# Pass one of a two-layer FFT-attention block: plain fp32 transforms in row halves of the array, one more pipeline stage, softmax taps finished on GpSimd

## The reference

```python
def _autocorrelation(Q, K, V):            # H = 8 heads, per channel
    qf = jnp.fft.fft(q, axis=2)
    kf = jnp.fft.fft(k, axis=2)
    corr = jnp.fft.ifft(qf * jnp.conj(kf), axis=2).real
    w, idx = jax.lax.top_k(corr.transpose(0, 1, 3, 2), 8)   # int(2 * log(64)) = 8 lags
    w = jax.nn.softmax(w, axis=-1)
    for i in range(8):
        g = jnp.minimum(idx[:, :, None, :, i] + pos, L - 1)
        out = out + w[:, :, None, :, i] * jnp.take_along_axis(v, g, axis=2)
...
x = x + _L0_xattn_ref(_layernorm(x), ctx, ctx)
x = x + _L0_ffn_ref(_layernorm(x), lora_A, lora_B, W, bias, lora_weights)   # W plus 8 LoRA adapters
x = x + _L1_xattn_ref(_layernorm(x), ctx, ctx, ...)  # grouped softmax attention
x = x + _L1_ffn_ref(_layernorm(x), ...)              # MLP plus routed low-rank experts
```

## Time and profile before

| | |
|---|---|
| three runs | 796.23, 796.25 and 799.37 us, median 796.25 |
| profiled execution | span 795.4 us, 13302 instructions; a time of its own is not listed, the median lies 0.85 us above the span |
| busy over the span | TensorE 91%, VectorE 66%, ScalarE 65%, GpSimd 44% |
| pass one | 0 to 273 us |
| first Q transforms of tiles 0, 1, 2, 3 | start at 9.56, 35.92, 64.39 and 77.94 us |
| DMA | 45.93 MB, 58 GB/s over the span, up to 401 GB/s in 2 us slices at the start |

### The profile page before, as it was taken

How to read it: one execution, slowest core, us unless ns; L and a number is a source line. 1 busy time by engine, 2 the same in 40 slices (tenths; PEclk the granted TensorE clock), 3 DMA queues, 4 the chain that set the end, 5 groups by cost and what they waited for, 6 DMA issues and landing times.

```text
span 795.4 us, 13302 instructions
## 1 busy us (share of the span) xinstructions
PE 727.3 (91%) x4048; PEld 550.2 (69%) x4048; DVE 521.6 (66%) x1265; ACT 520.6 (65%) x953; POOL 348.6 (44%) x430
## 2 busy tenths in 40 slices
PE   3779999999998765889999999999999999999983
PEld 2546767676765553667778778788788788786772
DVE  3367999999998346656666666666666665665422
ACT  4446786767674377867867867867867866866110
POOL 3054684444442214334544544544544544535323
PEclk9799999999999968999999999999999999999998
DMA  6751433232212221011011011011011011000000
GB/s 169 232 93 41 146 120 94 66 92 66 92 59 74 73 76 62 32 40 36 19 54 37 16 53 40 13 53 40 13 53 40 13 53 40 22 19 14 14 14 27
DMA packets 30464, 45.93 MB, mean 58 GB/s; under 512 B 7488, under 2 KB 9792, under 8 KB 30432
## 3 DMA queue, kind: packets, MB, share of 16 engines
q1 hardware_dynamic: 30432, 45.53, 19.1%
HBM read 37.13 MB, written 8.39 MB: 57 GB/s over the span
## 4 chain that ended last, share of the span: by engine, by line
PE 82%; DVE 5%; ACT 4%; issue 4%; POOL 1%; DMA 1%; SPq 0%; POOLq 0%; DVEq 0%; ACTq 0%
PE bank L1036 14%; PE bank L1038 13%; PE bank L1037 13%; PE wide L1036 6%; PE wide L1038 5%; PE wide L1037 5%; PE bank L1245 3%; PE wide L1134 3%; PE bank L1109 3%; PE wide L1335 2%; PE bank L1269 2%; PE wide L1146 2%; DMA gate_raw<-in_L_ffn_gate_w 1%; PE bank L1225 1%; PE wide L1199 1%
## 5 line engine op out<-in xcount | busy, mean ns | idle before, releaser
L636 POOL TENSOR_TENSOR va<-mv,small 128x1 f32<-128x1 f32 x80 | 15.3, 192 | 211.0 <-DVE mv L1016 98.4
L428 ACT ACTIVATE q_stack<-qt_h 32x512 fp32r<-32x512 f32 x128 | 80.6, 630 | 1.9
L1036 PE MATMUL bank<-down_h,ht_h 128*128 128x512 f32 x128 | 53.6, 419 | 4.8 <-DVE ht_l L940 3.4
L948 DVE RECIPROCAL y<-bank 128x256 f32<-128x256 f32 x32 | 56.0, 1751 | 0.0
L706 POOL TENSOR_TENSOR kbd_b<-kt_h,small 128x512 bf16<-128x512 f32 x32 | 34.1, 1088 | 48.0 <-ACT kt_h L550 48.0
L971 DVE TENSOR_TENSOR x<-bank,x_res 128x512 f32<-128x512 f32 x16 | 11.1, 692 | 66.9 <-PE bank L1038 66.9
L1036 PE MATMUL wide<-up_h,t_h 128*128 128x512 f32 x128 | 53.0, 414 | 1.1 <-DVE t_l L927 1.1
L720 POOL TENSOR_TENSOR y_l<-y,y_h 128x512 fp32r<-128x512 f32 x16 | 20.6, 1290 | 72.9 <-ACT y_h L580 72.9
L1037 PE MATMUL wide<-up_l,t_h 128*128 128x512 f32 x128 | 51.2, 400 | 0.0
L1038 PE MATMUL wide<-up_h,t_l 128*128 128x512 f32 x128 | 51.1, 400 | 0.0
L1038 PE MATMUL bank<-down_h,ht_l 128*128 128x512 f32 x128 | 51.0, 398 | 0.0
(11 more groups left out here) (217 smaller groups left out, 2361.5 us busy)
## 6 DMA issues: line engine op xcount, KB each, us to landing
ctx_t<-in_ctx SPq DMA_DIRECT2D x32, 256.0 KB, 2.8
x_in<-in_x SPq DMA_DIRECT2D x16, 256.0 KB, 2.7
x_res<-in_x SPq DMA_DIRECT2D x16, 256.0 KB, 3.4
x_rows<-x SPq DMA_DIRECT2D x16, 256.0 KB, 3.5
x_in<-x_rows SPq DMA_DIRECT2D x16, 256.0 KB, 2.6
x_res<-x_rows SPq DMA_DIRECT2D x16, 256.0 KB, 3.5
out<-stage SPq DMA_DIRECT2D x16, 256.0 KB, 2.0
stage<-in_L_ffn_up_w SPq DMA_DIRECT2D x2, 1024.0 KB, 4.9
```

The costliest lines, as they stand in the source:

```text
L428: last = act.activation(out[STACK * part:STACK * (part + 1), p, :], halves[STACK * p:STACK * (p + 1), :].bitcast(F32), ACT.Copy)
L948: dve.reciprocal(y[:, :, b, :], part[:, 1]).then_inc(S["den_s"], 1)
L1036: pe.matmul(out_ps, w_hi, m_hi, start=start, stop=False)
```

## The change

Pass one is written anew around these edits; pass two keeps its code.

- **Transforms.** `transform` becomes two plain fp32 matmuls, one for each sequence: sequence b has its data and its DFT matrix on rows 64b to 64b+63 and writes a PSUM bank of its own. Q, K, V and W need one such pair each. The splits x_h, x_l, c_h, c_l, wt_h, wt_l, dft_h, dft_l are gone, and so are the second K transform and the block-diagonal matrices. Q and W write ps_a, K and V write ps_b (two banks each). qf, prod and prod2 are instructions over both sequences, 1024 or 2048 wide. corr is eight matmuls of 64 columns in place of eight of 128.
- **One stage more.** x1(i) instead of x1(i+1) is made in body(i), the FFN is that of i-1, x2 is finished and stored in body(i) for tile i-2. x1 gets three buffers, x2 and vf two. The loop is unrolled and runs to NT+1.
- **Taps on GpSimd.** `match_replace` writes 0 over the kept weights after exp; GpSimd subtracts this from the weights and multiplies by 1/total.
- **Residual and bias.** x2 = FFN + x1 + b0 is two adds on GpSimd; the identity matmul and x1b are gone.
- **Loads.** ctx_t is read by the transforms themselves: SP loads tile i+3 in body(i) after v_ps. The order of SP's body is now: store of x2(i-2), x_res(i+1), x_in(i+4), weights, ctx_t(i+3).
- **Weights.** The host hands over W, fc1, expert_w and the LoRA matrices transposed and laid out, and the LoRA loads (four in place of fourteen) go out first. w0 = W.T (loaded) + A x B on VectorE; rt is split over bodies -1 and 0.

The diff, cut to its core:

```diff
 # SP
+            sp.dma_start(a_raw[:], lora_a).then_inc(S["lora_in"], 16)
+            sp.dma_start(b_raw[:], lora_bt).then_inc(S["lora_in"], 16)
+            sp.dma_start(coef[:], lora_w).then_inc(S["lora_in"], 16)
+            sp.dma_start(w0_sum[:], w0_t.rearrange("(c p) o -> p c o", p=P)).then_inc(S["lora_in"], 16)
...
             def body(i):
                 if early(i):
                     load2(0)
+                t = i - 2
+                if live(t):
+                    sp.wait_ge(S["x2_s"], t + 1)
+                    sp.dma_start(rows(x2_rows, t), x2s[t % 2][:]).then_inc(x2_stored[t % 2], 16)
                 t = i + 1
                 if live(t):
                     wait(sp, S["x1_s"], t)
                     sp.dma_start(x_res[:], rows(x_rows, t)).then_inc(S["res_loaded"], 16)
-                t = i - 1
-                if live(t):
-                    sp.wait_ge(S["x2_s"], t + 1)
-                    sp.dma_start(rows(x2_rows, t), x2[:]).then_inc(S["x2_stored"], 16)
...
-                    sp.wait_ge(S["x_hi"], t)
+                    sp.wait_ge(S["xn1_s"], t)
                     sp.dma_start(x_in[:], rows(x_rows, t)).then_inc(S["x_loaded"], 16)
...
-                t = i + 4
-                if live(t):
-                    sp.wait_ge(S["c_lo"], t)
+                t = i + 3
+                if live(t) and t > 0:
+                    sp.wait_ge(S["v_ps"], t)
                     sp.dma_start(ctx_t[:], rows(ctx_rows, t)).then_inc(S["ctx_loaded"], 16)
 # TensorE
-                return split_product(out_ps[:], dft_h[:, w], dft_l[:, w], hi[:], lo[:], True, True)
+                for b in range(2):
+                    k = slice(SEQ * b, SEQ * (b + 1))
+                    last = pe.matmul(out_ps[:, D * b:D * (b + 1)], dft[k, col:col + P], src[k, :], start=True, stop=True)
+                return last
...
+                t = i + 2
+                    pe.wait_ge(S["xn1_s"], t + 1)
+                    wait(pe, S["prod2_s"], t - 1)
+                    transform(ps_a, Q0, xn1).then_inc(S["q_ps"], 1)
+                    pe.wait_ge(S["ctx_loaded"], 16 * (t + 1))
+                    wait(pe, S["vsw_s"], t)
+                    transform(ps_b, K0, ctx_t).then_inc(S["k_ps"], 1)
+                # o(i); corr(i+2); transposes of wgt(i+1); V(i+2); W(i+1); FFN(i-1); transposes of xn2(i)
 # ScalarE, in this order: x1t_h(i-1), qf(i+2), wt(i+1), xn2(i), a weight's cast, vf(i+2),
 # exp(i+2), xn1(i+3), two half-partition copies of vf(i+2) (vsw_s), x2(i-1) (x2_raw)
 # GpSimd
             def body(i):
+                t = i + 1
+                if live(t):
+                    pool.wait_ge(S["rep_s"], t + 1)
+                    pool.wait_ge(S["exp_s"], t + 1)
+                    wait(pool, S["wt_ps"], t)
+                    pool.tensor_tensor(wgt[:], weight[:, :, 0:SEQ], kept_not[:], ALU.subtract).then_inc(S["sub_s"], 1)
+                    pool.wait_ge(S["sub_s"], t + 1)
+                    pool.wait_ge(S["inv_s"], t + 1)
+                    pool.tensor_tensor(wgt[:], wgt[:], total_inv[:].unsqueeze(2).to_broadcast([P, 2 * DC, SEQ]), ALU.mult
+                                       ).then_inc(S["wgt_s"], 1)
+                t = i
+                if live(t):
+                    wait(pool, S["xn2_s"], t)
+                    normaliser(t, mv2, va2, rs2, nm2, nb2, 2)
+                t = i + 3
+                if live(t):
+                    wait(pool, S["xn1_s"], t)
                     normaliser(t, mv1, va1, rs1, nm1, nb1, 1)
                 if staged_before(i):
                     low_half(i - 1, 0)
                     low_half(i - 1, 1)
...
+                t = i - 2
+                if live(t):
+                    x2_t = x2s[t % 2]
+                    pool.wait_ge(S["x2_raw"], t + 1)
+                    pool.tensor_tensor(x2_t[:], x2_t[:], x1[t % 3][:], ALU.add).then_inc(S["x2_res"], 1)
+                    pool.wait_ge(S["x2_res"], t + 1)
+                    pool.tensor_tensor(x2_t[:], x2_t[:], b0_all[:], ALU.add).then_inc(S["x2_s"], 1)
 # VectorE, in this order: match_replace, total, total_inv of i+1; prod(i+2); x1t_l(i-1);
 # x1(i), bn_stats, bn_aggr; bn_stats, bn_aggr of x_in(i+3); max, shift of i+2; prod2(i+1)
+                    w = ps_a[:].rearrange("p (b n) -> p b n", b=2).unsqueeze(2).to_broadcast([P, 2, 2, D])
+                    dve.tensor_tensor(prod2[:], w, vf[t % 2][:].rearrange("p j b n -> p b j n"), ALU.mult
+                                      ).then_inc(S["prod2_s"], 1)
```

More of the change, by code:

```diff
@@ new lines, in body @@
+                    for c in range(2 * DC):
+                        top = dve.max(m8[:, c, :], corr[:, c, :])
+                    top.then_inc(S["tops_s"], 1)
+                    dve.wait_ge(S["tops_s"], t + 1)
+                    wait(dve, S["sub_s"], t)
+                    best = m8[:, :, 0:1]
+                    dve.tensor_tensor(weight[:, :, 0:SEQ], corr, best.to_broadcast([P, 2 * DC, SEQ]), ALU.subtract)
+                    dve.tensor_tensor(weight[:, :, SEQ:], m8[:], best.to_broadcast([P, 2 * DC, TOP]), ALU.subtract
+                                      ).then_inc(S["shift_s"], 1)
@@ L1102, in body @@
-                t = i + 2
-                if live(t):
-                    pe.wait_ge(S["prod_s"], 2 * (t + 1))
-                    wait(pe, S["rep_s"], t)
-                    for c in range(DC):
-                        k = slice(c * P, (c + 1) * P)
-                        for j in range(2):
-                            last = pe.matmul(bank[4][:, k], prod[:, j, k], icorr[j], start=(j == 0), stop=(j == 1))
-                    last.then_inc(S["corr_ps"], 1)
-                    transform(bank[V_BANK[0]], V0, c_h, c_l).then_inc(S["v_ps"], 1)
+                    pe.wait_ge(S["xn1_s"], t + 1)
@@ L1116, in body @@
-                    for c in range(DC):
-                        last = pe.transpose(bank[5][:, c * P:(c + 1) * P], xn2[:, c * P:(c + 1) * P], ident)
-                    last.then_inc(S["xt_ps"], 1)
-                if early(i):
-                    turn_context(0)
-                if early(i, 1):
-                    queries(0)
-                t = i + 2
-                if live(t):
-                    transform(bank[V_BANK[1]], V0 + P, c_h, c_l).then_inc(S["v_ps"], 1)
-                t = i + 1
@@ L1136, in body @@
                     last.then_inc(S["o_ps"], 1)
+                t = i + 2
+                if live(t):
+                    pe.wait_ge(S["prod_s"], t + 1)
+                    wait(pe, S["shift_s"], t)
+                    for c in range(DC):
+                        for b in range(2):
+                            k = slice(P * c + SEQ * b, P * c + SEQ * (b + 1))
+                            last = pe.matmul(bank[4][:, k], prod[:, b, P * c:P * (c + 1)], icorr, start=True, stop=True)
+                    last.then_inc(S["corr_ps"], 1)
@@ new lines, in body @@
+                t = i + 1
+                if live(t):
+                    pe.wait_ge(S["wgt_s"], t + 1)
+                    wait(pe, S["xt_lo"], i)
+                    for c in range(DC):
+                        last = pe.transpose(cols(bank[5], c, P), wgt[:, 2 * c:2 * c + 2, :].rearrange("p b s -> p (b s)"),
+                                            ident)
+                    last.then_inc(S["wt_ps"], 1)
+                t = i + 2
+                if live(t):
+                    transform(ps_b, V0, ctx_t).then_inc(S["v_ps"], 1)
@@ new lines, in body @@
+                if early(i, 1):
+                    queries(0)
+                t = i + 1
+                if live(t):
+                    pe.wait_ge(S["wt_s"], t + 1)
+                    wait(pe, S["qf_s"], min(t + 2, NT))
+                    transform(ps_a, W0, wt).then_inc(S["wf_ps"], 1)
+                t = i - 1
+                if live(t):
+                    pe.wait_ge(S["xt_lo"], t + 1)
+                    wait(pe, S["x2_raw"], t)
+                    if t == 0:
+                        pe.wait_ge(S["w0_lo"], DC)
+                        pe.wait_ge(S["rt_lo"], DC)
+                    for c in range(DC):
+                        last = split_product(bank[7], cols(x1t_h, c, P), cols(x1t_l, c, P),
+                                             cols(w0_h, c, D), cols(w0_l, c, D), c == 0, c == DC - 1)
+                    last.then_inc(S["ffn_ps"], 1)
@@ L1145, in body @@
-                    pe.wait_ge(S["x1b_s"], t + 1)
-                    pe.matmul(bank[7][:], ident, x1b[:], start=False, stop=True).then_inc(S["ffn_ps"], 1)
-                if early(i):
-                    keys_values(0)
-                if isinstance(i, int) and i == -2:
-                    pe.wait_ge(S["lora_in"], 16 * (2 + DC + ADAPT))
-                    for c in range(DC):
-                        last = pe.transpose(bank[6][:, c * P:(c + 1) * P], b_raw[:, c, :], ident)
-                    last.then_inc(S["bt_ps"], 1)
@@ L1154, in body @@
[L1154 to L1160 removed]
```

(2 more changed lines are left out.)

544 lines of the change are left out of this document (215 added, 329 removed).

## The result

The changed kernel takes 862.1 us (859.96 to 866.08 in 4 runs) against 797.7 us before in the same comparison (796.23 to 799.37): ratio 1.082, 95% interval 1.079 to 1.085. It is slower, by more than I had forecast (843), inside the range. The profiled execution has a span of 858.0 us against 795.4.

What follows compares the result with a forecast made beforehand. The prediction took TensorE to bound pass one before, and a ring through the context load, held behind the x2 store, after. Its terms, -10.9 + 26.8 + 26.2 + 5.1 = +47.2 on a 795.4 us span, gave 843 us, range 808 to 866.

Steps and rivals of the forecast that it cites:

- The wait and its ring: Steady pass one: the context load waits behind the x2 store for GpSimd's adds; K to K 14.5 us, bounds 14.1 and 15.0.
- D: Pass one: loads don't hold K, VectorE and ScalarE set 12.2 us a tile; time 769, chance 0.12.
- C: Transforms on TensorE: row halves take turns, K grows by 0.85 or 1.7 us; time about 861, chance 0.11.
- The tile step: Tiles 7 to 15 of pass one: 16.2 us each against 13.29, +26.2 us in all (bounds +7 and +38).
- B: Pass one: the ring holds but TensorE's clock stays up behind the gap; time 820, chance 0.26.
- Term 1: Start to the end of tile 3's K transform: 69.2 us against 80.15, -10.9 (bounds -20 and -5).
- wt 30.9: Link in the start's chain: wt of the first tile, after GpSimd's taps at 29.6, is ready at 30.9 us.
- Term 2: Tiles 4 to 6, casts and low halves ahead of the x2 adds: 66.7 us against 39.9, +26.8 (bounds +15 and +30).
- Term 4: From tile 15's K transform to pass two: 38.8 us against 33.7, +5.1, for the added stage.
- o(15) behind the FFN of 13 and the keys of pass two, and the queries: Between tile 15's K transform and pass two: o(15) queued behind this work, 7.5 us.
- FFN of 15 and its copy 5: Between tile 15's K transform and pass two: split, FFN of tile 15 and its copy take 5 us.
- TensorE's work: Pass one, each tile: some 10.6 us on TensorE (14.0 at the other end) against 13.3, with corr at half its columns.

Runs made afterwards that it cites:

- gap filled: Changed kernel with three pairs of extra plain fp32 matmuls on TensorE ahead of its wait for the context load: 848.2 us.
- the load free: Changed kernel with the context load moved from last to first in SP's body, ahead of the store of x2: 786.7 us.
- the store behind all loads: Changed kernel with the context load first in SP's body and the store of x2 behind x_res, x_in and the staged weights: 779.8 us.
- the best kernel here: Changed kernel with context load first, store last, qf copied earlier, pass two's query bias add after x1(15), and x2(15) made by one VectorE add: 766.0 us.

## Why the prediction held, and where it was off

- **The wait and its ring: right.** Store behind the second add, 1.4 us of issues, landing, K, o, x1, statistics, two normalisers, two adds: each link stands in the trace in that order. At the full clock (gap filled) three steps are 14.7 to 14.8, against a sum of 14.5; the mean of nine is 15.5, for the reasons given there.
- **D (the loads don't hold K) was the only rival on the faster side. It was out, as I had argued, and its step was right once its condition was made true.** With the load free the steady step is 12.06; I had written 12.2, from VectorE and ScalarE. Its total was 18 us too low, 769 against 787: K(3) comes at 62.8, not 57.5, tiles 4 to 6 take 45.1, not 41.5, and the tail 43.6, not 38.
- **C (row halves take turns): out.** A pair costs 0.97.
- **The tile step, 16.2 against 16.58: near, but by luck in its parts, since two errors cancel.** I put the slow clock into most tiles, 1.7 each, with a landing of 3.1. The landing was too short: from issue to K's start the nine loads of tiles 7 to 15 took 3.3, 5.2, 3.2, 5.1, 4.2, 3.3, 3.8, 3.3 and 3.1, on average 3.8 (the 3.6 that I had bounded it with, in the earlier trace rows, is that of a store). The clock was priced too high: o was slow (3.2 to 3.7 in place of 1.94) in five of the nine, and what the slow K and o take beyond 1.13 and 1.94 us comes to 1.1 us a tile (an estimate from their rows). Behind the gap of 3.0 us at 157.4 the clock stayed up, behind the 4.95 at 172.1 it fell: a landing that late lengthens its own turn, and the next o ran on the slow level. B (the clock stays up) was therefore half true of the tiles and false of the time.

The windows of the changed kernel in and behind two gaps, as in the earlier trace rows:

```profile
173.00:177.00 4.00, 0.00 (x0) 0.00 (x0) 0.00 (x0) 0.70 (x1) 1.13 (x2) 0.83 0.45 152
177.10:183.90 6.80, 6.80 (x24) 2.53 (x24) 2.95 (x4) 0.00 (x0) 0.00 (x0) 0.60 0.00 0
191.50:194.40 2.90, 0.00 (x0) 0.00 (x0) 0.00 (x0) 1.54 (x3) 1.87 (x2) 1.00 0.79 266
194.40:199.00 4.60, 4.59 (x27) 2.46 (x27) 3.22 (x5) 0.00 (x0) 0.00 (x0) 1.00 0.00 0
```

- **Term 1, the start, 5.5 us too early: the failed step is the chain up to "wt 30.9".** wt(0) is copied at 35.80 to 36.40, and the low halves of wq end at 42.96, where I had 37.6. Three links make it up. The load of w0, with the LoRA loads, lets ScalarE go on at 12.07, not at 10, so prod(0) ends at 15.2, not 13.3: 1.9 us. corr(0) then runs at a granted clock of 0.50 and takes 3.67 us, where I had 1.9 for the full clock: 1.8. The copies, w0's halves and the taps keep that delay (the taps end at 33.38, not 29.6). And I followed ScalarE's and GpSimd's queues and left out TensorE's own, in which corr(1) stands ahead of the transposes of wgt(0) until 35.15: 1.7. The rest of the chain, 31.6 us in the forecast, took 31.7:

```profile
15.25 3.67 PE L1068 MATMUL bank<-first,prod 128*128 128x64 f32 x16 [4.02 <-DVE prod L786]
...
35.15 0.61 PE L1075 MATMUL bank<-small,wgt 128*128 128x128 f32 x4
...
52.92 2.08 PE L1036 MATMUL ps_b<-ctx_t,dft 64*128 64x512 f32 x4 [10.55 <-DMA ctx_t<-in_ctx]
```

```profile
42.98 4.05 SPq L350 DMA_DIRECT2D stage<-in_L_xattn_Wo  x8
47.08 0.42 SPq L354 DMA_DIRECT2D ctx_t<-in_ctx  x1
```

- **Term 2, +30.1 against +26.8, just over its bound of +30** (+30.6 against the 39.9 that I had for before). The three steps are 18.3, 28.6 and 23.6 against 18.7, 25.75 and 22.2. The mechanism is confirmed from both sides: moving the weights alone gives back 11 us, moving the store alone 14.6; the first also takes some landing with it, so the two are not parts of one sum. (With everything out of the way of the load, as in "the store behind all loads", 29.8 are gone.) The missing 2.9 of tile 5: o(2) slow throughout (3.68), 0.8 more than I had; the landing 7.8 (111.52 to 119.35) in place of 6.2, 1.6; K at a granted clock of 0.50, 0.4.
- **Term 4, 42.0 against 38.8: the failed steps are "o(15) behind the FFN of 13 and the keys of pass two, and the queries" and "FFN of 15 and its copy 5".** I let the queries delay o(15) on TensorE. They stand behind it there, and it is VectorE's add to them that holds x1(15) for 3.6 us; by the forecast's sum x1(15) begins at 319.9, in the trace at 322.3. The FFN of tile 15 then runs mostly at a granted clock of 0.50 (329.3 to 332.6), and from its transposes to the end of its copy 6.7 us pass, not 5. Moving the add and shortening the last x2 took 5.7 us off.
- **TensorE's work, 10.6 against 11.5 a tile: corr was mis-sized, at about half its time.** It did not matter behind a ring of 14.5; it is the bound of the best kernel here.
- **Where the gain went.** By work alone this is a faster kernel, as I wrote: with the load free it runs at 12.06 a tile against 13.29. The other reorderings bring it to 11.5 and the total to 766, 3.9% under the kernel before.

## What to carry to other kernels

A queue that issues loads in order must not hold a store that waits for the last instruction of a tile ahead of a load that the same tile's first instruction needs; ask of every wait in such a queue what is behind it and when that is due. Put loads first in the order of their due time, or give the buffer a twin, either is enough. Before pricing a stage at the start or the end of a pipeline, follow every engine's queue through it, also those of which the step seems to need nothing: at both ends of this forecast an instruction that I had left out stood ahead of the one that I followed, and the slow clock fell on matmuls that I had priced at the full one.

## What the hardware showed that I had not expected

- Halving the columns of a plain fp32 matmul from 128 to 64 saved nothing: corr's sixteen records take 1.84 us from their start to the next instruction's with 64 columns, and took 1.70 with 128 (161.64 to 163.34 in the kernel before). Each has a weight load of its own beside it (193 ns in the mean from 145 to 290 us, 192 in the kernel before). The Trainium skill's "TensorE: Matmul & The Clock Gate", Back-to-back issue gap, says that the spacing in a stream of weight loads and matmuls is set by both. The rows are consistent with that; no run here varies the loads alone, nor shows why 64 columns take 0.14 us more.
- Two plain fp32 matmuls on rows 0 to 63 and 64 to 127 cost 0.97 us together and 1.82 on the same rows, the change of form included.
- Of the nine gaps of tiles 7 to 15, the three of 4.1 to 5.0 us all had the slow o behind them, of the six of 2.3 to 3.4 us two had. So a gap's length alone does not tell whether TensorE falls from 2.4 to 1.2 GHz.
- The same load, as the last of a bunch of four, took 3.2 to 5.2 us from issue to K's start, with nothing else in the queue.
